# A vision tower's block on one core: gathers issued ahead of GpSimd's adds and powers, second norms' statistics ahead of the low parts, the biases' load in four parts

## The chip, the cores and the metric

One core of one Trainium2 chip runs the kernel as one launch. The metric is the device time of one execution in microseconds (us). The engines are TensorE (PE), VectorE (DVE), ScalarE (ACT), GpSimd (POOL) and SyncE (SP), which only issues transfers here. Times with a decimal such as 541.53 are moments, in us from the start of the profiled span.

## The reference

```python
h = L0_tok_ref(x, ...)                       # 8 x 256 x 512, a state space model's kernel
h = concat([cls_tok, h], axis=1)             # 8 batches of 257 rows of 512
h = h + attention(layernorm(h), ...)         # 16 heads of 32
h = h + ffn(layernorm(h), ...)

def ffn(x, router_w, router_b, expert_w, expert_b, out_w, out_b):
    probs = softmax(x @ router_w + router_b)            # 8 experts
    top, idx = top_k(probs, 2); top = top / top.sum()
    expert_out = gelu(x @ expert_w[e] + expert_b[e])    # for every e, 512 x 512
    combined = sum over the two chosen experts of gate * expert_out
    return combined @ out_w + out_b
```

Only the two chosen experts of a row matter, so the kernel computes those alone.

## The kernel before

The kernel makes the tokens, runs attention for 8 batches one after another, and then the experts. Rows are kept as 17 token tiles of 128 rows: two halves for each of 8 batches, and one class tile whose first 8 rows are the class rows. Matrix products in float32 precision are made of three passes of TensorE: an operand is split into a high part (a rounded copy, made by ScalarE) and a low part (the operand less its high part, made by VectorE); `ew_hi` and `ew_lo` are those of the experts' matrices, `xnT_hi` and `xnT_lo` those of a turned (transposed) tile.

**Slot tiles.** Each row appears twice, once for each of its experts, in a list sorted by expert and padded to 40 tiles of 128 slots. The kernel doesn't wait for the last two batches: the first 16 slot tiles (`FULL`) hold only rows of the first six batches, whose routing is done within attention's last batch. Then for slot tile i: GpSimd gathers its rows from `xn_dram` (`gather(i)`, L917) into one of two buffers, TensorE turns them (`turn_xs(i)`, L2492), ScalarE makes the high part (`hi_xs`, L1335), the low part comes from VectorE (`lo_xs`, L1999) for tiles 0, 1 and from 8 on and from ScalarE (`lo_xs`, L1346, out of a difference that TensorE makes, `rest_of_xs`, L2247) for tiles 2 to 7, TensorE multiplies by the expert's matrix (`expert(i)`, L2313), ScalarE applies gelu (L1356) and issues the store. For tiles 0 to 11 TensorE adds the expert's bias by a matmul (L2790) of picked rows of `bias_rows`; later tiles get it from VectorE out of `eb`, a copy of all biases on all partitions (2 MB, loaded by SyncE, L676). `bias_rows` itself comes from a small load `bias_rows_raw` (L670), ScalarE's high part (L1367) and VectorE's low part (L2023), followed by the picks (L2025).

**The late token tiles.** Tiles of the last two batches and the class tile (numbers 12 to 16 in TensorE's order) are finished beside the first slot tiles: VectorE adds attention's output (`residual`, L1669; class rows L2030), makes the second norm's statistics (`stats_of`, `norm_sums`, L1672 to L1678; class tile L2048 to L2052), GpSimd takes the power -1/2 (`norm_pow`, L895; class tile L938) and adds the output bias into `h_ob` (`last_bias`, L891; class tile L940) for SyncE to store (`keep_h`, L639; class tile L683), and VectorE normalises in place (`normalise`, L1684; class tile L2060), which must come behind that add. SyncE stores the normalised tiles (`keep_xn`, L644; class tile L685). TensorE turns them (`turn_xn`) behind expert tile 3, ScalarE copies them (`keep_xnT`, L1175), and routing of the rest follows from there, spread over slot tiles 4 to 14 by tile number. The low parts of experts 1 to 7 (`lo_expert`, L1995) are made by VectorE in between: expert 1's behind the statistics of batch 6, expert 2's behind the class tile's, expert 3's behind the normalising of batch 7, experts 4 to 7 at the end.

**What sets the order.** Every engine runs its own program in the order written, and semaphores are the only links. The lists that matter here:

- TensorE: turn 0, turn 1, expert 0, turn 2, expert 1, turn 3, expert 2, turn 4, expert 3, turns of late tiles 12 to 16, turn 5, expert 4, logits of the late tiles, turn 6, expert 5 and so on. In the middle of expert i (for i up to 6) comes `rest_of_xs(i + 1)`, which waits for ScalarE's high part of tile i + 1.
- GpSimd before: add for batch 6 (two), gathers 0 and 1, power of batch 6, gathers 2 and 3, adds for batch 7 (two), power of batch 7, class power, class add, two fills, gathers 4 to 39. A gather i waits until tile i - 2 is turned.
- ScalarE: high parts of tiles 0 and 1, high part of the bias rows, high parts of experts 5 to 7, gelu of tile 0; then for each tile i: high part of i + 1, store of i - 1, low part of i + 1, gelu of i. Behind gelu 3 it copies late tiles 12 to 15, waits for the stores out of `h_ob`, the class tile's among them, and copies tile 16, whose place overlaps `h_ob`; only then comes the high part of tile 5.

```python
                if i == 3:
                    for n in range(EARLY_TILES, NT - 1):
                        keep_xnT(n)
                    act.wait_ge(st_h[0], 16 * (NB + 2))
                    act.wait_ge(st_h[1], 16 * (NB + 1))
                    keep_xnT(NT - 1)
```

- SyncE: matrix of expert 7, `h_ob` of batch 7 (two stores), the biases `eb`, normalised tiles of batches 6 and 7 (four stores), class tile's `h_ob`, class tile's normalised rows. All of these use one queue.

Of the kernel before, what the change touches and what calls it, by code (L numbers as in the profile page):

```python
# [8 lines left out]
ALU = mybir.AluOpType  # L9
# [3 lines left out]
P = 128  # L13
BANK = 512
EPS = 1e-5
# [6 lines left out]
def vit_tower_kernel(nc, x, cls_tok, log_dt, B_ri, inv_A_real, A_imag, Wq, bq, Wk, bk, Wv, bv, Wo, bo,  # L22
# [69 lines left out]
    BIASES_BY_PE = 12  # L92
    DVE_KEPT = [sum(KEPT_BY_DVE[:n]) for n in range(NT + 1)]
# [15 lines left out]
    with ExitStack() as whole:  # L109
# [457 lines left out]
        def _(sp):  # L567
# [105 lines left out]
            for st in range(HALVES):  # L673
                keep_h(last, st)
            sp.wait_ge(s["dve_bias_rows"], 1)
            sp.dma_start(eb[:, :, :].rearrange("p e d -> p (e d)"),  # L676
                         expert_b.rearrange("e d -> (e d)").rearrange("(a n) -> a n", a=1).broadcast_to([P, NE * D])
                         ).then_inc(s["loaded_biases"], 16)
# [35 lines left out]
        def _(pool):  # L714
# [178 lines left out]
            def norm_pow(m):  # L893
                pool.wait_ge(s["dve_stats2"], 5 * m + 5)
                pool.tensor_tensor(rs2[:, 1, :], rs2[:, 0, :], mhalf[:, :], ALU.pow).then_inc(s["pool_rstd"], 1)  # L895
# [33 lines left out]
            for i in range(2):  # L929
                gather(i)  # L930
            norm_pow(last - 1)
            for i in range(2, 4):
                gather(i)
            for st in range(HALVES):
                last_bias(last, st)
            norm_pow(last)
            pool.wait_ge(s["dve_stats2"], 5 * NB + 3)
            pool.tensor_tensor(rsc[:, 1, :], rsc[:, 0, :], mhalf[:, :], ALU.pow).then_inc(s["pool_rstd"], 1)  # L938
            pool.wait_ge(st_h[0], 16 * (NB + 1))
            pool.tensor_tensor(h_ob[:, 0, :], tok[:, CLS, :], ob[:, :], ALU.add).then_inc(s["pool_out_bias"], 1)  # L940
            pool.wait_ge(s["pe_cls_projected"], 1)
# [3 lines left out]
            for i in range(4, FULL):  # L945
                gather(i)
# [19 lines left out]
        def _(act):  # L966
# [453 lines left out]
        def _(dve):  # L1420
# [250 lines left out]
            def residual_stats(m, st):  # L1671
                dve.bn_stats(st2[:, st, :], tok[:, st * NB + m, :]).then_inc(s["dve_stats2"], 1)  # L1672

            def norm_sums(m):
                for st in range(HALVES):
                    dve.bn_aggr(mv2[:, st, :], st2[:, st, :]).then_inc(s["dve_stats2"], 1)
                dve.wait_ge(s["dve_stats2"], 5 * m + 4)
                dve.tensor_scalar(rs2[:, 0, :], mv2[:, :, 1], EPS, None, ALU.add).then_inc(s["dve_stats2"], 1)  # L1678

            def normalise(m, st):  # L1680
# [1211 lines left out]
```

## Time and profile before

| | |
|---|---|
| median of 3 runs | 752.23 us (751.95 to 752.47) |
| profiled execution, as timed | 749.79 us |
| its span in the profile | 748.0 us |
| TensorE busy | 675.2 us, 90% of the span |
| VectorE busy | 526.9 us, 70% |
| ScalarE busy | 417.1 us, 56% |
| GpSimd busy | 158.0 us, 21% |
| granted TensorE clock, mean | 0.977 of full speed |

The profiled execution is one of its own, timed at 749.79 us, 2.44 less than the median of the runs; all moments in this document are within its span of 748.0 us. A row of a timeline gives the start, the duration (of all instructions merged in it, if it says x2 or more), the engine, the line, the operation, what it writes and reads, and in brackets how long the engine was idle before it and what ended that. L917 is line 917 of the kernel. Matmuls are pipelined, so the distance between two starts says more than a duration.

### The profile page before, as it was taken

To read this page: it belongs to the slowest core of one execution; us is meant where nothing else is said; L and a number is where in the kernel's file an instruction comes from. 1 tells how busy PE (TensorE), PEld (TensorE's weight loads), DVE (VectorE), ACT (ScalarE), POOL (GpSimd) and SP (SyncE) were. 2 spreads that over 40 slices of the span, in tenths; PEclk is the share of its full clock that TensorE was granted. 3 is DMA by queue.
4 is the path that set the end of the run, shared out by engine and by line. 5 is a ranking of instruction groups with operands and counts; after the bars stand their busy time and mean duration, and the time that the engine had idled before them with its cause. 6 is when DMAs were issued, how large, how long until landed. Compare 5 with 4: busy or idle time off the path is not lost.

```text
span 748.0 us, 16610 instructions
## 1 busy us (share of the span) xinstructions
PE 675.2 (90%) x5699; PEld 539.0 (72%) x5700; DVE 526.9 (70%) x1240; ACT 417.1 (56%) x1077; POOL 158.0 (21%) x310
## 2 busy tenths in 40 slices
PE   4788988879999999999999999796769989998998
PEld 3577877768777787877778787564557778886886
DVE  7999883657777787787878777867842744446775
ACT  5864644577767676676667667755433423334111
POOL 5200000110120201212111120111822232236660
PEclk9889999989999999999999999999889999999999
DMA  7501255300000010000001002426543356666895
GB/s 204 193 1 29 114 143 143 72 1 2 3 29 28 14 42 0 28 28 28 28 14 42 0 28 86 169 71 218 187 172 120 120 151 208 202 188 207 262 331 173
DMA packets 54684, 76.29 MB, mean 102 GB/s; under 512 B 24729, under 2 KB 27033, under 8 KB 54514
## 3 DMA queue, kind: packets, MB, share of 16 engines
q1 hardware_dynamic: 40978, 42.56, 17.8%
q0 software_dynamic: 5920, 19.40, 9.4%
q10 hardware_dynamic: 7744, 13.77, 5.0%
q8 instruction: 26, 0.43, 0.2%
q14 instruction: 16, 0.13, 0.1%
HBM read 45.55 MB, written 30.16 MB: 101 GB/s over the span
## 4 chain that ended last, share of the span: by engine, by line
PE 68%; DVE 16%; ACT 5%; issue 4%; DMA 3%; POOL 2%; ACTq 0%; DVEq 0%; POOLq 0%; SPq 0%
PE ps L2313 41%; PE ps L2419 8%; PE ps L2429 4%; PE ps L2412 4%; PE ps L2492 3%; DVE ring L1578 3%; DVE ring L1577 3%; ACT prb L1135 2%; PE ps L2260 1%; DMA rows_in<-xn_dram,token_of 1%; PE ps L2436 1%; PE ps L2291 1%; DVE prb L1657 1%; PE ps L2304 1%; PE ps L2379 1%
## 5 line engine op out<-in xcount | busy, mean ns | idle before, releaser
L1135 ACT ACTIVATE prb<-ps,negmax 128x257 f32<-128x257 f32 x256 | 117.7, 479 | 4.7 <-DVE negmax L1648 3.7
L1648 DVE TENSOR_REDUCE negmax<-ps 128x2 f32<-128x514 f32 x128 | 82.4, 685 | 13.5 <-PE ps L2412 13.5
L2419 PE MATMUL ps<-ident,prb 128*128 128x128 f32 x512 | 83.4, 286 | 9.4 <-DVE prb L1657 3.4
L2419 PEld LDWEIGHTS ps<-ident,prb 128*128 128x128 f32 x512 | 57.0, 143 | 33.9 <-issue 10.7
L1657 DVE TENSOR_SCALAR prb<-prb,rrec 128x258 f32<-128x258 f32 x256 | 73.5, 351 | 2.3
L2313 PE MATMUL ps<-ew_hi,xnT_hi 128*128 x160 | 68.5, 428 | 3.9 <-DVE xnT_lo L1999 3.4
L1356 ACT ACTIVATE rows_out<-ps 128x512 f32<-128x512 f32 x40 | 23.9, 598 | 79.0 <-DVE ps L2068 60.2
L2313 PE MATMUL ps<-ew_lo,xnT_hi 128*128 x160 | 64.7, 404 | 0.0
L2313 PE MATMUL ps<-ew_hi,xnT_lo 128*128 x160 | 64.3, 402 | 0.0
L917 POOL DMA_INDIRECT rows_in<-xn_dram,token_of x40 | 40.7, 1018 | 107.9 <-PE ps L2492 88.9
L1999 DVE TENSOR_TENSOR xnT_lo<-ps,xnT_hi 128x512 fp32r<-128x512 f32 x34 | 23.5, 690 | 55.9 <-ACT xnT_hi L1335 55.7
L1143 ACT ACTIVATE pts_far<-ps 128x512 f32<-128x512 f32 x64 | 38.6, 604 | 41.8 <-PE ps L2419 41.8
L2260 PE MATMUL ps<-ident,ring 128*128 128x128 f32 x384 | 49.3, 286 | 7.3 <-DVE ring L1578 7.2
L1135 ACT ACTIVATION_READ_ACCUMULATOR prb<-ps,negmax 128x1 f32 x256 | 53.9, 211 | 0.0
L2260 PEld LDWEIGHTS ps<-ident,ring 128*128 128x128 f32 x384 | 44.9, 148 | 11.5 <-DVE ring L1578 11.2
L2492 PE MATMUL ps<-ident,rows_in 128*128 128x128 f32 x228 | 35.5, 279 | 16.5 <-DMA rows_in<-xn_dram,token_of 13.4
L1654 DVE RECIPROCAL rrec<-rowsum 128x4 f32<-128x4 f32 x64 | 11.4, 178 | 52.8 <-ACT prb L1135 52.5
L2492 PEld LDWEIGHTS ps<-ident,rows_in 128*128 128x128 f32 x228 | 27.4, 142 | 25.7 <-DMA rows_in<-xn_dram,token_of 13.6
L848 POOL TENSOR_TENSOR pcls<-prb,ones 128x12 f32<-128x12 f32 x40 | 8.4, 209 | 149.4 <-DVE prb L1657 149.4
L2313 PEld LDWEIGHTS ps<-ew_hi,xnT_hi 128*128 128x128 f32 x160 | 31.5, 197 | 10.8 <-issue 5.1
L2313 PE MATMUL ps<-xT_hi,wqT_hi 128*128 128x258 f32 x128 | 38.7, 303 | 0.0
L959 POOL DMA_INDIRECT y_rows<-y_slots,slot_of x34 | 34.8, 1024 | 17.7 <-DVE rows_in L2209 10.5
(480 smaller groups left out, 1812.3 us busy)
## 6 DMA issues: line engine op xcount, KB each, us to landing
y_slots<-rows_out ACTq DMA_DIRECT2D x40, 256.0 KB, 3.4
ew<-in_L_ffn_expert_w_dram SPq DMA_DIRECT2D x8, 1024.0 KB, 5.5
h_dram<-h_ob SPq DMA_DIRECT2D x17, 256.0 KB, 2.0
xn_dram<-tok SPq DMA_DIRECT2D x17, 256.0 KB, 2.2
h_late<-h_dram SPq DMA_DIRECT2D x12, 256.0 KB, 4.5
out_dram<-h_late SPq DMA_DIRECT2D x11, 256.0 KB
y_slots<-u_sb SPq DMA_DIRECT2D x9, 256.0 KB, 5.7
tok_dram<-so SPq DMA_DIRECT2D x4, 512.0 KB, 3.2
```

The source lines that it names most:

```text
L917: pool.indirect_dma_start(out=rows_in[:, i % 2, :], out_offset=None, in_=xn_dram[0:rows, :], in_offset=bass.IndirectOffsetOnAxis(ap=token_ ...
L959: pool.indirect_dma_start(out=y_rows[:, t % Y_RING, k, :], out_offset=None, in_=y_slots, in_offset=bass.IndirectOffsetOnAxis(ap=slot_of[:, ...
L1135: e = act.activation(prb[:, u % 2, j, 0:KEYS], ps[:, j, 0:KEYS], ACT.Exp, bias=negmax[:, u % 2, j:j + 1], accum_out=rowsum[:, u % 2, j:j + 1])
L1143: act.activation(pts(slot, 2)[:, :, :, st * P:(st + 1) * P], ps[:, 4, :].rearrange("p (h t s) -> p h t s", h=2, t=HALVES), ACT.Copy).then_ ...
L1648: dve.tensor_reduce(negmax[:, u % 2, 2 * b:2 * b + 2], ps[:, 2 * b:2 * b + 2, 0:KEYS], AX_X, ALU.max, negate=True).then_inc(s["dve_max"], 1)
L1657: e = dve.tensor_scalar(prb[:, u % 2, j, :], prb[:, u % 2, j, :], rrec[:, u % 2, j:j + 1], None, ALU.mult)
L2260: mm = pe.matmul(ps[:, n % 4, q * P:(q + 1) * P], part(q), ident[:, :], is_transpose=True, start=(k == 0 and q == 0), stop=(k == len(parts ...
L2313: mm = pe.matmul(out_ap, a, b, start=start and i == 0, stop=stop and i == 2, skip_group_check=skip)
L2412: mm = pe.matmul(ps[:, j, 0:KPAD], a[rows, ci, st * P:(st + 1) * P], b[rows, ci, :], start=(a is q_hi and b is k_hi), stop=(b is k_lo))
L2419: mm = pe.transpose(ps[:, 4, (2 * j + tt) * P:(2 * j + tt + 1) * P], prb[:, u % 2, 2 * b + j, tt * P:(tt + 1) * P], ident[:, :])
L2429: mm = pe.matmul(ps[j * DH:(j + 1) * DH, bank, 0:KEYS], v_sb[:, tt, h * DH:(h + 1) * DH], pts(h)[:, 0, tt, 0:KEYS], start=(tt == 0), stop= ...
L2492: mm = pe.matmul(ps[:, bank, k * P:(k + 1) * P], src[:, k * P:(k + 1) * P], ident[:, :], is_transpose=True, start=(k == 0), stop=(k == KC ...
```

## The change

- GpSimd issues gathers 2 and 3 directly behind 0 and 1, then does batch 7's adds, then both batches' powers and the class power; gathers 4 and 5 follow ahead of the class add, 6 and 7 behind it, ahead of the two fills. The class add now waits for `dve_attn_done` itself.
- Batch 7's statistics get tiles of their own (`lnst`, `lnmv`, `lnr`), so that they needn't wait for batch 6's normalising.
- VectorE makes the low parts of tiles 0 and 1 (and adds the class rows) ahead of the biases' low part and the picks; then the statistics of batch 6, of batch 7 and of the class tile; then the low parts of experts 1 to 7; then it normalises batch 6, batch 7 and the class tile.
- ScalarE makes the high part of the bias rows ahead of tiles 0 and 1.
- SyncE loads `eb` in four parts of two experts each; part n (from 0) waits until n + 3 slot tiles are turned.

```diff
+    BIASES_AT_ONCE = 2
...
             sp.wait_ge(s["dve_bias_rows"], 1)
-            sp.dma_start(eb[:, :, :].rearrange("p e d -> p (e d)"),
-                         expert_b.rearrange("e d -> (e d)").rearrange("(a n) -> a n", a=1).broadcast_to([P, NE * D])
-                         ).then_inc(s["loaded_biases"], 16)
+            for e in range(0, NE, BIASES_AT_ONCE):
+                sp.wait_ge(s["pe_slot_turned"], 3 + e // BIASES_AT_ONCE)
+                some = expert_b[e:e + BIASES_AT_ONCE, :].rearrange("e d -> (e d)").rearrange("(a n) -> a n", a=1)
+                sp.dma_start(eb[:, e:e + BIASES_AT_ONCE, :].rearrange("p e d -> p (e d)"),
+                             some.broadcast_to([P, BIASES_AT_ONCE * D])).then_inc(s["loaded_biases"], 16)
...
             pool.wait_ge(s["dve_token_of"], 1)
-            for i in range(2):
-                gather(i)
-            norm_pow(last - 1)
-            for i in range(2, 4):
+            for i in range(4):
                 gather(i)
             for st in range(HALVES):
                 last_bias(last, st)
-            norm_pow(last)
+            norm_pow(last - 1)
+            norm_pow(last, lnr)
             pool.wait_ge(s["dve_stats2"], 5 * NB + 3)
             pool.tensor_tensor(rsc[:, 1, :], rsc[:, 0, :], mhalf[:, :], ALU.pow).then_inc(s["pool_rstd"], 1)
+            gather(4)
+            gather(5)
             pool.wait_ge(st_h[0], 16 * (NB + 1))
+            pool.wait_ge(s["dve_attn_done"], 1)
             pool.tensor_tensor(h_ob[:, 0, :], tok[:, CLS, :], ob[:, :], ALU.add).then_inc(s["pool_out_bias"], 1)
+            gather(6)
+            gather(7)
             pool.wait_ge(s["pe_cls_projected"], 1)
...
-            for i in range(4, FULL):
+            for i in range(8, FULL):
                 gather(i)
...
+            act.wait_ge(s["loaded_biases"], 16 * 2 * DH // NE)
+            act.activation(bias_rows[0:2 * DH, :], bias_rows_raw[0:2 * DH, :], ACT.Copy).then_inc(s["act_w_high"], 1)
             act.wait_ge(s["dve_expert_of"], 1)
             hi_xs(0, 0, True)
             hi_xs(1, 1, True)
-            act.wait_ge(s["loaded_biases"], 16 * 2 * DH // NE)
-            act.activation(bias_rows[0:2 * DH, :], bias_rows_raw[0:2 * DH, :], ACT.Copy).then_inc(s["act_w_high"], 1)
...
             for st in range(HALVES):
                 residual(last, st, 2 + st)
+            lo_xs(0, 0)
+            dve.wait_ge(s["loaded_cls"], 16)
+            dve.wait_ge(s["pe_cls_projected"], 1)
+            dve.tensor_tensor(tok[0:NB, CLS, :], ps[0:NB, 6, :], tok[0:NB, CLS, :], ALU.add).then_inc(s["dve_attn_done"], 1)
+            lo_xs(1, 1)
             dve.wait_ge(s["act_w_high"], KC * KC + 1)
...
-            lo_xs(0, 0)
-            dve.wait_ge(s["loaded_cls"], 16)
-            dve.wait_ge(s["pe_cls_projected"], 1)
-            dve.tensor_tensor(tok[0:NB, CLS, :], ps[0:NB, 6, :], tok[0:NB, CLS, :], ALU.add).then_inc(s["dve_attn_done"], 1)
-            lo_xs(1, 1)
...
-            stats_of(last - 1)
-            norm_sums(last - 1)
-            lo_expert(1)
-            for st in range(HALVES):
-                normalise(last - 1, st)
-            stats_of(last)
-            dve.wait_ge(s["dve_xn"], 2 * last)
-            norm_sums(last)
+            stats_of(last - 1, own_sums)
+            dve.wait_ge(s["dve_stats2"], 5 * last)
+            stats_of(last, last_sums)
+            dve.wait_ge(s["dve_stats2"], 5 * NB)
             dve.wait_ge(s["dve_attn_done"], 1)
             dve.bn_stats(stc[:, :], tok[:, CLS, :]).then_inc(s["dve_stats2"], 1)
...
-            lo_expert(2)
+            for e in range(1, NE):
+                lo_expert(e)
             for st in range(HALVES):
-                normalise(last, st)
-            lo_expert(3)
+                normalise(last - 1, st, own_sums)
+            for st in range(HALVES):
+                normalise(last, st, last_sums)
             dve.wait_ge(s["pool_rstd"], NB + 1)
             dve.wait_ge(s["pool_out_bias"], NT)
             dve.tensor_scalar(tok[:, CLS, :], tok[:, CLS, :], mvc[:, 0:1], rsc[:, 1, 0:1], ALU.subtract, ALU.mult
                               ).then_inc(s["dve_xn"], 1)
-            for e in range(4, NE):
-                lo_expert(e)
...
-            dve.wait_ge(s["loaded_biases"], 16 * 2 * DH // NE + 16)
+            dve.wait_ge(s["loaded_biases"], 16 * 2 * DH // NE + 16 * NE // BIASES_AT_ONCE)
```

## Rows read from the trace of the kernel before

**Rows 1.** The page: its first line, and one line of the transfers issued.

```profile
span 748.0 us, 16610 instructions
...
h_dram<-h_ob SPq DMA_DIRECT2D x17, 256.0 KB, 2.0
```

**Rows 2.** The chain that ended last, 510 to 565 us: start, us, what.

```profile
525.90 2.70 POOL rs L895
...
534.73 2.66 POOL rsc L938
537.39 3.72 POOL h_ob L940
...
541.53 6.20 DMA rows_in<-xn_dram,token_of
```

**Rows 3.** Timeline of TensorE.

```profile
523.19 0.79 PE L2313 MATMUL ps<-ew_hi,xnT_hi 128*128 x1 [2.96 <-DVE xnT_lo L1999]
...
547.77 1.12 PE L2492 MATMUL ps<-ident,rows_in 128*128 128x128 f32 x4 [5.44 <-DMA rows_in<-xn_dram,token_of]
...
554.49 1.10 PE L2492 MATMUL ps<-ident,tok 128*128 128x128 f32 x8
...
557.80 0.60 PE L2492 MATMUL ps<-ident,rows_in 128*128 128x128 f32 x4
...
561.53 0.49 PE L2790 MATMUL ps<-bias_rows,picks 64*128 64x512 f32 x1
```

**Rows 4.** Timeline of VectorE.

```profile
521.41 0.68 DVE L2023 TENSOR_TENSOR bias_rows<-bias_rows_raw,bias_rows 32x512 fp32r<-32x512 f32 x1 [4.71 <-ACT bias_rows L1367]
...
529.62 1.28 DVE L1672 BATCH_NORM_STATS2 st<-tok 128x6 f32<-128x512 f32 x2
...
531.21 2.42 DVE L1678 TENSOR_SCALAR rs<-mv 128x2 f32<-128x2 f32 x1
...
534.55 2.29 DVE L1995 TENSOR_TENSOR ew_lo<-ew,ew_hi 128x2048 fp32r<-128x2048 f32 x1
536.75 1.00 DVE L1684 TENSOR_SCALAR tok<-tok,mv,rs 128x512 f32<-128x512 f32 x2
537.66 2.29 DVE L1995 TENSOR_TENSOR ew_lo<-ew,ew_hi 128x2048 fp32r<-128x2048 f32 x1
...
541.67 8.89 DVE L1995 TENSOR_TENSOR ew_lo<-ew,ew_hi 128x2048 fp32r<-128x2048 f32 x4
```

**Rows 5.** Timeline of ScalarE.

```profile
520.27 0.60 ACT L1335 ACTIVATE xnT_hi<-ps 128x512 fp32r<-128x512 f32 x1 [0.77 <-PE ps L2492]
...
521.28 5.50 ACT L1248 ACTIVATE ew_hi<-ew 128x2048 fp32r<-128x2048 f32 x3
526.80 1.28 ACT L1356 ACT_TABLE_LOAD   x1
...
558.08 0.60 ACT L1175 ACTIVATE xnT_cls<-ps 128x512 f32<-128x512 f32 x1 [0.40 <-PE ps L2492]
```

**Rows 6.** Timeline of GpSimd.

```profile
530.12 0.95 POOL L917 DMA_INDIRECT rows_in<-xn_dram,token_of  x1 [0.30 <-issue]
531.10 2.50 POOL L891 TENSOR_TENSOR h_ob<-tok,ob 128x512 f32<-128x512 f32 x2
...
537.35 3.75 POOL L940 TENSOR_TENSOR h_ob<-tok,ob 128x512 f32<-128x512 f32 x1
...
542.96 1.83 POOL L917 DMA_INDIRECT rows_in<-xn_dram,token_of  x1 [0.30 <-issue]
```

**Rows 7.** Stretches: length, then each engine's busy time, granted clock, DMA share, GB/s.

```profile
512.00:514.00 2.00, 0.84 (x25) 0.77 (x26) 1.90 (x11) 1.22 (x1) 0.00 (x0) 1.00 1.04 395
...
548.00:550.00 2.00, 2.00 (x7) 1.54 (x7) 2.00 (x2) 0.60 (x1) 0.84 (x1) 0.50 0.15 58
```

**Rows 8.** Timeline of SyncE's queue.

```profile
534.00 0.45 SPq L676 DMA_DIRECT2D eb<-in_L_ffn_expert_b_dram  x1
```

**Rows 9.** Line 683, the class tile's store of h, issued at 541.13: time to landing.

```profile
DMA to landing us min/median/max: 6.5/6.5/6.5
```

More of the change, by code:

```diff
@@ L891, in add_bias, with norm_pow @@
                 pool.tensor_tensor(h_ob[:, st, :], tok[:, st * NB + m, :], ob[:, :], ALU.add).then_inc(s["pool_out_bias"], 1)
-            def norm_pow(m):
+            def norm_pow(m, sums=rs2):
                 pool.wait_ge(s["dve_stats2"], 5 * m + 5)
-                pool.tensor_tensor(rs2[:, 1, :], rs2[:, 0, :], mhalf[:, :], ALU.pow).then_inc(s["pool_rstd"], 1)
+                pool.tensor_tensor(sums[:, 1, :], sums[:, 0, :], mhalf[:, :], ALU.pow).then_inc(s["pool_rstd"], 1)
             body(0, True)
@@ L1669, in residual, with residual_stats, norm_sums, normalise @@
                 dve.tensor_tensor(t, ps[:, bank, :], t, ALU.add).then_inc(s["dve_residual"], 1)
-            def residual_stats(m, st):
-                dve.bn_stats(st2[:, st, :], tok[:, st * NB + m, :]).then_inc(s["dve_stats2"], 1)
-            def norm_sums(m):
+            own_sums, last_sums = (st2, mv2, rs2), (lnst, lnmv, lnr)
+            def residual_stats(m, st, sums=own_sums):
+                dve.bn_stats(sums[0][:, st, :], tok[:, st * NB + m, :]).then_inc(s["dve_stats2"], 1)
+            def norm_sums(m, sums=own_sums):
                 for st in range(HALVES):
-                    dve.bn_aggr(mv2[:, st, :], st2[:, st, :]).then_inc(s["dve_stats2"], 1)
+                    dve.bn_aggr(sums[1][:, st, :], sums[0][:, st, :]).then_inc(s["dve_stats2"], 1)
                 dve.wait_ge(s["dve_stats2"], 5 * m + 4)
-                dve.tensor_scalar(rs2[:, 0, :], mv2[:, :, 1], EPS, None, ALU.add).then_inc(s["dve_stats2"], 1)
-            def normalise(m, st):
+                dve.tensor_scalar(sums[2][:, 0, :], sums[1][:, :, 1], EPS, None, ALU.add).then_inc(s["dve_stats2"], 1)
+            def normalise(m, st, sums=own_sums):
                 dve.wait_ge(s["pool_out_bias"], 2 * m + st + 1)
@@ L1683, in normalise @@
                 t = tok[:, st * NB + m, :]
-                dve.tensor_scalar(t, t, mv2[:, st, 0:1], rs2[:, 1, st:st + 1], ALU.subtract, ALU.mult
+                dve.tensor_scalar(t, t, sums[1][:, st, 0:1], sums[2][:, 1, st:st + 1], ALU.subtract, ALU.mult
                                   ).then_inc(s["dve_xn"], 1)
@@ L2026, in _, with stats_of @@
                               ALU.is_equal).then_inc(s["dve_bias_rows"], 1)
-            lo_xs(0, 0)
-            dve.wait_ge(s["loaded_cls"], 16)
-            dve.wait_ge(s["pe_cls_projected"], 1)
-            dve.tensor_tensor(tok[0:NB, CLS, :], ps[0:NB, 6, :], tok[0:NB, CLS, :], ALU.add).then_inc(s["dve_attn_done"], 1)
-            lo_xs(1, 1)
-            def stats_of(m):
+            def stats_of(m, sums):
                 for st in range(HALVES):
                     dve.wait_ge(s["dve_residual"], HALVES * m + 1 + st)
-                    residual_stats(m, st)
+                    residual_stats(m, st, sums)
                 dve.wait_ge(s["dve_stats2"], 5 * m + 2)
-            stats_of(last - 1)
-            norm_sums(last - 1)
-            lo_expert(1)
-            for st in range(HALVES):
-                normalise(last - 1, st)
-            stats_of(last)
-            dve.wait_ge(s["dve_xn"], 2 * last)
-            norm_sums(last)
+                norm_sums(m, sums)
+            stats_of(last - 1, own_sums)
+            dve.wait_ge(s["dve_stats2"], 5 * last)
+            stats_of(last, last_sums)
+            dve.wait_ge(s["dve_stats2"], 5 * NB)
             dve.wait_ge(s["dve_attn_done"], 1)
```

## The prediction

> **What bounds the kernel now.** I read the chain of waits first, then each engine's timeline in the stretch where attention ends and the expert tiles begin, then the transfers. The profiled execution spans 748.0 us [rows 1]. From 563 us on, the chain is TensorE with pauses that hang on tile numbers; what is decided before that point shifts the end by itself. Up to 563 the chain isn't TensorE: it goes through GpSimd, whose power waits for VectorE's statistics and runs 2.70 us, whose class power runs 2.66 and whose class add runs 3.72, and then through gather 4, which takes 6.20 from its issue at 541.53 to TensorE's turn [rows 2]. TensorE stands idle for 5.44 in front of that turn, at 547.77. Tile 0 also starts late, at 523.19 after 2.96 of idleness, for want of its low part [rows 3]; VectorE makes that only after the biases' low part of 521.41, for which it had waited 4.71 [rows 4].
>
> I use one mark: the end of expert tile 4. Its bias matmul starts at 561.53 and the next work comes 0.42 later: **561.95** [rows 3]. The gain at the mark is the gain at the end.
>
> **Part 1, gathers first.** Gather 2 needs only that tile 0 is turned, and was held by the power until 528.6 [rows 2]. Now gathers 2 and 3 go at about 519.0 and 520.5 (tile 1 was turned by 520.2, since ScalarE copied it at 520.27 [rows 5]) and land before TensorE asks. Each costs GpSimd 0.95. Their price is that the last two adds, 2.50 together [rows 6], now sit at 521.5 to 524.0.
>
> **Part 2, the biases' copy ahead of the tiles' high parts on ScalarE, the tiles' low parts ahead of the biases' on VectorE.** The bias rows' small loads stood behind two matrices that still ran at 395 GB/s between 512 and 514 [rows 7]; I count them as there by 516, so the copy (0.6) fits in before tile 0 is turned at 518.8. Were they 2 us later, tile 0's high part would slip by up to 0.6, which the slack below swallows. Tile 0 then starts near 520.4, 2.8 earlier. Tile 1's second half needs tile 2's high part, and ScalarE comes to that only after three matrices (5.50, from 520.8), a table load (1.28) [rows 5] and one copy: 528.7. So tile 1 ends near 531 and tile 2 near 534.6. Tile 3 needs gather 4, which now stands behind the class power: about 537. It ends near 541.2, against 554.49 before [rows 3]: 13 us won so far. It doesn't last.
>
> **Part 3, statistics first, then all seven low parts, then the normalising.** TensorE's next work behind tile 3 is to turn the five late token tiles, which must be normalised; VectorE now does that after the low parts of experts 1 to 7. VectorE is ready for the biases' low part at 521.5, the very moment at which GpSimd's adds start. What a meeting costs: a 128x2 operation issued at 531.21 took 2.42, until GpSimd's two adds of 531.10 were over [rows 4, 6]. I take the like of it: free at 524.0. Then the biases' low part and the picks, 0.8; two rounds of statistics at 1.7 (a pair of 1.28 and what follows, 529.62 to 531.21 and a last step); the class tile, 0.9 (533.63 to 534.55) [rows 4]. The low parts begin at **529.1**; without a meeting, at 526.7. Four low parts took 8.89 and one takes 2.29, so one follows another after 2.20 [rows 4]; seven take 15.5: **544.6**. The first normalised tile is 0.5 later (two take 1.00) [rows 4], 545.1. Five turns and that of slot tile 5 took from 554.49 to 558.40, 3.9. TensorE comes out of 4 us of idleness; behind such a pause one turn took 1.12 instead of 0.60 [rows 3] and the granted clock was 0.50, 1.2 GHz, in the stretch from 548 to 550 [rows 7]. I add 1.0 in all (bounds 0 and 2): tile 5 is turned at **550.0**.
>
> **Part 4, the biases' load in four parts.** The 2 MB load was issued at 534.00 [rows 8] and slowed everything behind it: the class tile's store of h took 6.5 [rows 9] where such a store takes 2.0 [rows 1]. The parts now wait for turned slot tiles 2 to 5, and SyncE's order is otherwise kept: part four, four normalised tiles, the class tile's h, its normalised rows. So **those five stores wait, with part four, for tile 5's turn at 550.0**. ScalarE waits for the class store of h before it copies the fifth late tile (the copy's place overlaps h_ob), and in its program the high part of slot tile 5 comes after that copy; TensorE needs that high part in the middle of expert tile 4. Before, this wait cost nothing: the store had landed at 547.6 (541.13 + 6.5) and the copy of 558.08 waited for its turn alone [rows 5, 9]. Now, from 550.0: 0.52 + 4 x 0.26 + 0.26 MB and gather 7's 0.26 are 2.1 MB, at 395 GB/s [rows 7] 5.3 us, and 1.7 for issue and start (a lone store of 0.26 MB lands in 2.0 [rows 1], 0.65 of it at that rate). That is 7.0: **557.0**. Bounds 5.0 (the rate alone) and 8.5. Two copies of 0.6 [rows 5]: 558.3. The rest of tile 4 takes 2.1 at the full clock (half of the 4.15 from 557.80 to the mark) and 3.4 at the low one (a turn and tile 3 took 6.7 behind a pause, 547.77 to 554.49, so 2.6 more, half of it here) [rows 3]; I take 2.8: **561.1**.
>
> **The sum.** 529.1 + 15.5 + 5.4 + 7.0 + 1.3 + 2.8 = 561.1 against 561.95: 0.85 off. The profiled execution took 749.79 as timed; the median of the runs is 752.23, 2.4 more, and I subtract from the median: **751.4**. The early gain is nearly all given back.
>
> **Bounds of the sum.** Low: no meeting (2.4), transfers in 5.0 (2.0), full clock (0.7 and 1.0): 745.3. High: the class add gets in between two low parts and holds VectorE for 1.25 (half of 2.50 [rows 6]), the class power for 0.6 (it ended at 537.39, behind a low part that ended at 536.84 [rows 2, 4]), transfers 8.5, low clock 0.6 more: 755.3.
>
> **A rule of the skill against the trace.** Two rows show who waits at the port that VectorE and GpSimd share. The class add of 537.35 took 3.75, until 1.15 behind the end of a low part that started after it, at 537.66: it was passed over. Gather 5, issued at 542.96 during a low part, ended at 544.79, 0.9 behind the start of the next one at 543.87 (541.67 + 2.20) [rows 4, 6]: it got in. The Trainium skill, SBUF — State Buffer, "Who interferes with whom", says that a VectorE instruction with two SBUF inputs and a GpSimd one that reads SBUF exclude each other and that whoever issues first gets the ports, and it infers that a tensor_tensor doesn't hold up a gather's descriptors. By it a waiting power is let in at the next boundary, the third rival below has no chance, and the time is 751.4. The trace agrees on the exclusion, not on the order; and for the gather it shows 1.83 instead of 0.95 where the page infers no wait.
>
> **Rivals.**
> 1. *SyncE's order doesn't reach TensorE.* If the class store landed in time, tile 4 would run from 550.0 and end near 554: 8 gained, **744.2**. For it: the wait never showed before. Against it: the order of the queue and of ScalarE's program. Chance 0.10.
> 2. *The same chain, but short:* GpSimd's adds miss VectorE (526.7) and the transfers take 6: **748.0**. For it: the two starts at 521.5 are within 0.1 of each other. Chance 0.17.
> 3. *The class power starves behind seven low parts, and gather 4 with it.* The power is issued just as the first low part begins, as at 534.73, where it took 2.66 [rows 2]. There it got in behind one low part; the add of 537.35 was passed over at its first boundary. Held until VectorE rests at 546.5: power 547.2, gather 4 issued by 548.4 and landed at 551.0, tile 3 until 555.2, turns 559.1, transfers 566.1, mark 570.2: 8.2 lost, **760.4**. TensorE wants gather 4 by 540.9 (4.2 ahead of 545.1), so this decides from a power that ends later than 537, behind the third low part. Chance 0.10. The milder case (the class add and a power let in between low parts, a slow queue: **755**) has 0.10 more.
> 4. *The change doesn't do what it says:* the stalls trade places exactly, within 1 us of **752.2**. Chance 0.08.
>
> **How the numbers follow.** A measurement of this kernel can tell about 0.2%, 1.5 us, from no change. My case has 0.45; its own range is 748.8 to 753.8, with 0.16 faster, 0.24 within, 0.05 slower. Rivals 1 and 2 add 0.27 to faster, rival 3 and its milder case 0.20 to slower, rival 4 0.08 to the same. Together: faster 0.43, same 0.32, slower 0.25. The range leaves out rival 1 and the starved case (0.20) and ends at the bounds, 745.3 and, rounded up, 756.
>
> **What would show it.** Right: gather 2 near 519 and no wait of 5 us for a gather at tile 3; VectorE with seven low parts in a row from 527 to 529; TensorE idle for about 4 us ahead of the late tiles' turns and again for 4 to 6 in the middle of expert tile 4, released by ScalarE's high part, which sits behind the copy that waits for the class store; SyncE's part four right behind tile 5's turn near 550. Wrong: no pause inside tile 4 (rival 1), a bias low part of 0.68 at 521.5 (rival 2), a class power of more than 8 us (rival 3). A mark under 555 or over 566 would mean that I follow the wrong chain.

## The result and the profile after

The median of 6 runs is **755.8 us** (754.46 to 757.23) against 752.09 for the kernel before in the same session (751.15 to 752.62, 6 runs): ratio **1.005, interval 1.0037 to 1.0063**. The change made the kernel 3.7 us slower; the forecast was 751.4 and somewhat faster. The profiled execution took 757.23, with a span of 755.5.

How TensorE waited tells the story in two answers. The list of TensorE's waits, before (514 to 562 us) and after (517 to 568); columns: who waited, for what, us in total, times, longest:

```profile
PE ps L2492 <- DMA rows_in<-xn_dram,token_of: 11.6, 4, 5.4
PE ps L2313 <- DVE xnT_lo L1999: 3.0, 1, 3.0
```

```profile
PE ps L2252 <- ACT xnT_hi L1341: 8.7, 2, 7.8
PE ps L2497 <- DVE tok L1692: 3.5, 1, 3.5
PE ps L2497 <- DMA rows_in<-xn_dram,token_of: 2.8, 2, 2.1
PE ps L2795 <- DVE picks L2038: 1.1, 1, 1.1
```

The waits for gathers fell from 11.6 to 2.8 and the one for a low part from 3.0 to 0.5. In their place stand 3.5 for the normalised tiles and 8.7 for a high part, 7.8 of it in one piece. The lines shown add up to 14.6 before and 16.1 after.

The chain that ended last, after:

```profile
524.71 2.98 DVE bias_rows L2036
...
534.68 7.88 DVE ew_lo L2003 x4
542.56 2.02 issue
544.58 4.48 DVE ew_lo L2003 x2
549.06 0.47 DVE tok L1692
...
551.07 3.57 PE ps L2497 x16
554.66 0.33 SPq L680
...
557.06 5.60 DMA h_dram<-h_ob
...
563.18 0.60 ACT xnT_hi L1341
```

GpSimd, which carried the chain before [rows 2], is gone from it; the 2.02 called issue at 542.56 lie within a low part that began at 541.28 and that GpSimd's class add had held up. The chain runs over VectorE's low parts, the late turns, SyncE's part four (554.66), the class tile's store and ScalarE's high part: the forecast's path, in the forecast's order. TensorE's timeline shows the moments on it:

```profile
523.85 0.49 PE L2318 MATMUL ps<-ew_hi,xnT_hi 128*128 x1 [0.53 <-DVE xnT_lo L2007]
...
540.26 0.85 PE L2497 MATMUL ps<-ident,rows_in 128*128 128x128 f32 x4 [2.14 <-DMA rows_in<-xn_dram,token_of]
...
549.66 1.07 PE L2497 MATMUL ps<-ident,tok 128*128 128x128 f32 x8 [3.47 <-DVE tok L1692]
...
553.82 0.81 PE L2497 MATMUL ps<-ident,rows_in 128*128 128x128 f32 x4
...
563.82 0.80 PE L2252 MATMUL ps<-xnT_hi,nident 128*128 128x512 f32 x1 [7.80 <-ACT xnT_hi L1341]
...
567.11 0.79 PE L2795 MATMUL ps<-bias_rows,picks 64*128 64x512 f32 x1
```

These answer to [rows 3]. Tile 3's turn, 547.77 before, is at 540.26, and the late turns, 554.49 before, at 549.66. Then, in the middle of tile 4, TensorE stands idle for 7.80. The mark (end of tile 4) is at 567.83. VectorE, ScalarE, GpSimd and SyncE [rows 4, 5, 6, 8, 9], one timeline each, then the landing of the class store (line 686):

```profile
524.71 2.98 DVE L2036 TENSOR_TENSOR bias_rows<-bias_rows_raw,bias_rows 32x512 fp32r<-32x512 f32 x1
...
532.48 16.58 DVE L2003 TENSOR_TENSOR ew_lo<-ew,ew_hi 128x2048 fp32r<-128x2048 f32 x7
```

```profile
562.68 0.60 ACT L1181 ACTIVATE xnT_cls<-ps 128x512 f32<-128x512 f32 x1 [9.04 <-DMA h_dram<-h_ob]
```

```profile
524.56 2.57 POOL L894 TENSOR_TENSOR h_ob<-tok,ob 128x512 f32<-128x512 f32 x2
...
532.64 2.66 POOL L939 TENSOR_TENSOR rsc<-rsc,mhalf 128x2 f32<-128x2 f32 x1 [0.45 <-DVE rsc L2057]
535.48 2.38 POOL L920 DMA_INDIRECT rows_in<-xn_dram,token_of  x1 [0.17 <-issue]
538.16 1.82 POOL L920 DMA_INDIRECT rows_in<-xn_dram,token_of  x1 [0.30 <-issue]
540.01 2.49 POOL L944 TENSOR_TENSOR h_ob<-tok,ob 128x512 f32<-128x512 f32 x1
542.65 2.83 POOL L920 DMA_INDIRECT rows_in<-xn_dram,token_of  x1 [0.15 <-issue]
```

```profile
529.16 25.83 SPq L680 DMA_DIRECT2D eb<-in_L_ffn_expert_b_dram  x4
555.03 1.99 SPq L645 DMA_DIRECT2D xn_dram<-tok  x4
557.06 0.43 SPq L686 DMA_DIRECT2D h_dram<-h_ob  x1
```

```profile
DMA to landing us min/median/max: 5.6/5.6/5.6
```

SyncE's fourth part ends its issue at 554.99, behind tile 5's turn; the class store waits its turn behind it and four stores of normalised tiles, and lands at 562.66. ScalarE's copy of the fifth late tile has waited 9.04 for that and starts at 562.68. The high part of tile 5, which TensorE wants, is next in ScalarE's program.

Stretches of after: length, busy time of TensorE, its weight loads, VectorE, ScalarE and GpSimd, granted clock, DMA share, GB/s.

```profile
551.00:553.00 2.00, 1.93 (x9) 1.66 (x10) 0.34 (x1) 1.01 (x2) 0.00 (x0) 0.50 0.00 0
...
555.00:557.00 2.00, 1.02 (x5) 0.50 (x3) 0.00 (x0) 0.00 (x0) 1.15 (x3) 1.00 0.67 152
...
559.00:561.00 2.00, 0.00 (x0) 0.00 (x0) 0.00 (x0) 0.00 (x0) 0.00 (x0) 1.00 1.03 398
561.00:563.00 2.00, 0.00 (x0) 0.00 (x0) 0.00 (x0) 0.32 (x1) 0.00 (x0) 0.52 0.80 307
...
565.00:567.00 2.00, 2.00 (x6) 1.17 (x4) 0.00 (x0) 0.25 (x1) 0.00 (x0) 0.50 0.04 8
...
612.00:614.00 2.00, 2.00 (x6) 1.55 (x6) 0.69 (x1) 0.24 (x1) 0.82 (x1) 0.57 0.59 172
```

The DMA engines are full only from 557 on. TensorE comes out of the pause with the granted clock at 0.50, which is 1.2 GHz, and the rest of tile 4 takes 4.0 (563.82 to 567.83). The last line is a later place where that clock shows.

**Where the time went.** The profiled executions differ by 7.5 us, more than the medians. I split each span at the start of gather 0 and at the mark:

| | ahead of gather 0 | gather 0 to mark (stage) | mark to end (tail) | span |
|---|---|---|---|---|
| before | 514.47 | 47.48 | 186.05 | 748.0 |
| after | 517.51 | 50.32 | 187.67 | 755.5 |
| before, second profile (e8) | 514.75 | 47.49 | 185.96 | 748.2 |
| after, second profile (e11) | 515.35 | 50.30 | 187.65 | 753.3 |

The stage and the tail repeat within 0.1. What lies ahead of gather 0 does not (512.6 to 517.6 over all thirteen profiles), and the change edits no instruction there; I take it for scatter (the section on e8 and e11 says how far that is shown). So the change costs **2.8 in the stage and 1.6 in the tail**. That is 4.4 to 4.5 in two profiles of each kernel, against 3.7 by the medians.

The 1.6 of the tail have one place. The distance from the turn of tile 16, which stands behind the wait for its gather (1.8 us in both kernels), to the next turn is 3.72 before (605.00 to 608.72) and 5.31 after (610.95 to 616.26). In after the granted clock fell to 0.57 there, as the last line above shows. TensorE's timelines, before and after:

```profile
605.00 0.66 PE L2492 MATMUL ps<-ident,rows_in 128*128 128x128 f32 x4 [1.75 <-DMA rows_in<-xn_dram,token_of]
```

```profile
610.95 0.66 PE L2497 MATMUL ps<-ident,rows_in 128*128 128x128 f32 x4 [1.80 <-DMA rows_in<-xn_dram,token_of]
```

### The profile page after: what moved, and what is told of

The parts are those of the page before. It is cut to its first block, busy times and chain, and to the rows that moved or that the text cites. A ratio compares the mean times of both kernels' runs of the same rounds, so it can differ in the third digit from the quotient of the medians.

```text
span 755.5 us, 16616 instructions
## 1 busy us (share of the span) xinstructions
PE 679.7 (90%) x5699; PEld 540.7 (72%) x5700; DVE 528.0 (70%) x1240; ACT 417.5 (55%) x1077; POOL 157.6 (21%) x310
## 4 chain that ended last, share of the span: by engine, by line
PE 68%; DVE 18%; ACT 5%; issue 4%; DMA 3%; POOL 1%; ACTq 0%; SPq 0%; DVEq 0%; POOLq 0%
PE ps L2318 41%; PE ps L2424 8%; PE ps L2434 4%; PE ps L2417 4%; PE ps L2497 4%; DVE ring L1583 3%; DVE ring L1584 3%; ACT prb L1141 2%; DVE ew_lo L2003 2%; PE ps L2441 1%; PE ps L2265 1%; PE ps L2296 1%; DVE prb L1663 1%; PE ps L2309 1%; PE ps L2384 1%
## 5 line engine op out<-in xcount | busy, mean ns | idle before, releaser
L920 POOL DMA_INDIRECT rows_in<-xn_dram,token_of x40 | 42.5, 1063 | 118.8 <-PE ps L2497 100.2
L2265 PE MATMUL ps<-ident,ring 128*128 128x128 f32 x384 | 47.7, 280 | 6.7 <-DVE ring L1584 6.7
L2265 PEld LDWEIGHTS ps<-ident,ring 128*128 128x128 f32 x384 | 43.0, 143 | 11.0 <-DVE ring L1584 10.7
L2497 PEld LDWEIGHTS ps<-ident,rows_in 128*128 128x128 f32 x228 | 27.5, 142 | 16.5 <-DMA rows_in<-xn_dram,token_of 5.6
L2318 PE MATMUL ps<-xT_hi,wkT_hi 128*128 128x258 f32 x128 | 39.0, 305 | 0.0
```

The costliest lines, as they stand in the source:

```text
L920: pool.indirect_dma_start(out=rows_in[:, i % 2, :], out_offset=None, in_=xn_dram[0:rows, :], in_offset=bass.IndirectOffsetOnAxis(ap=token_ ...
L2265: mm = pe.matmul(ps[:, n % 4, q * P:(q + 1) * P], part(q), ident[:, :], is_transpose=True, start=(k == 0 and q == 0), stop=(k == len(parts ...
L2318: mm = pe.matmul(out_ap, a, b, start=start and i == 0, stop=stop and i == 2, skip_group_check=skip)
L2497: mm = pe.matmul(ps[:, bank, k * P:(k + 1) * P], src[:, k * P:(k + 1) * P], ident[:, :], is_transpose=True, start=(k == 0), stop=(k == KC ...
```

## The experiments

Each ran beside the kernel before on the same chip; stage, tail and tile 16 are read from one profiled execution of each, the medians from 4 to 10 runs. The edits are against the kernel after unless it says "before". Nothing is left out of the computation in any. Medians and ratios (with interval) are against the kernel before of the same session, whose medians were 751.88 (e1 to e4), 751.77 (e5 to e8) and 751.47 (e9 to e11). The last column is the distance at tile 16.

| kernel | median | ratio | stage | tail | tile 16 |
|---|---|---|---|---|---|
| before | 752.09 | 1 | 47.48 | 186.05 | 3.72 |
| after | 755.80 | 1.0050 | 50.32 | 187.67 | 5.31 |
| e1 before, load in four parts | 757.28 | 1.0079 (1.0051 to 1.0106) | 54.25 | 186.65 | 3.71 |
| e2 no waits for the parts | 744.42 | 0.9902 (0.9877 to 0.9928) | 41.02 | 187.23 | 5.03 |
| e3 parts last | 746.76 | 0.9930 (0.9911 to 0.9950) | 41.45 | 186.16 | 3.71 |
| e4 normalising first | 747.68 | 0.9949 (0.9927 to 0.9971) | 42.68 | 187.69 | 5.31 |
| e5 both of these | 738.78 | 0.9836 (0.9805 to 0.9867) | 33.98 | 186.17 | 3.72 |
| e6 before, GpSimd's order | 747.29 | 0.9947 (0.9928 to 0.9966) | 42.45 | 185.73 | 3.71 |
| e7 e5, adds behind the picks | **736.17** | 0.9803 (0.9781 to 0.9825) | 33.55 | 185.98 | 3.72 |
| e9 class store first | 751.56 | 1.0004 (0.9982 to 1.0026) | 46.47 | 187.48 | 5.25 |
| e10 waits one tile earlier | 745.75 | 0.9919 (0.9894 to 0.9943) | 40.41 | 187.83 | 5.25 |

The theory: two orders bind in a row, VectorE's (seven low parts ahead of the normalising) and SyncE's (stores behind part four, which waits for tile 5's turn). Rivals: the waits cost nothing and the low parts do it all; the size of the load does it, not its wait; or the pause inside tile 4 comes of something else on ScalarE.

### e1: the four-part load alone, on the kernel before

```diff
+    BIASES_AT_ONCE = 2
...
-            sp.dma_start(eb[:, :, :].rearrange("p e d -> p (e d)"),
...
+            for e in range(0, NE, BIASES_AT_ONCE):
+                sp.wait_ge(s["pe_slot_turned"], 3 + e // BIASES_AT_ONCE)
...
```

> The kernel before with the four-part load of the biases alone, waits and all. The queue theory (the class tile's store of h waits on SyncE behind part four, part four waits for tile 5's turn, and ScalarE's high part of tile 5 waits for that store): tile 5's turn stays at 558.4, the store lands about 8.0 later, then 1.2 for copies and about 4 for the rest of tile 4, mark near 571.5 against 561.95, less what a lighter queue gives gather 4 (up to 2.5): 7 to 10 us slower, 759 to 762, with a pause of 6 to 8 us inside expert tile 4. The VectorE theory (the loss is in the low parts ahead of the normalising): no loss from this part, 752 or a little less.

Slower by 5.4 us in the median, 2 to 5 us less than expected; the stage is 6.8 longer, just under the expected 7 to 10, and the pause inside tile 4 is 7.98, as expected. SyncE's and ScalarE's timelines:

```profile
559.64 0.43 SPq L686 DMA_DIRECT2D h_dram<-h_ob  x1
```

```profile
565.61 0.60 ACT L1178 ACTIVATE xnT_cls<-ps 128x512 f32<-128x512 f32 x1 [9.12 <-DMA h_dram<-h_ob]
```

The same pause stands in a kernel whose VectorE and GpSimd orders are untouched. The split also brings something: with no 2 MB in the way, gather 4 was on TensorE 3.5 after its issue (543.61 to 547.12) instead of 6.2 [rows 2].

### e2: the parts without their waits

```diff
-                sp.wait_ge(s["pe_slot_turned"], 3 + e // BIASES_AT_ONCE)
```

> The changed kernel with its four loads issued at once, without waiting for turned tiles. Queue theory: the class store goes out when the class add is done, ten us ahead of its use, the pause of 7.8 us inside expert tile 4 is gone and with it the low clock behind it: 8 to 10 us faster than the changed kernel, 746 to 748. VectorE theory: the wait of 3.5 us for the late tiles is what costs, and it stays: 754 to 756.

The pause inside tile 4 is gone and the stage is 9.3 shorter. So the pause comes with the wait, not with the size of the load. The wait of 4.69 for the normalised tiles stays, as the theory says. The median is 2 to 4 us below what was expected. One link of the expectation was wrong: the class store didn't go out when the class add was done (542.50), ten us ahead of its use, but behind the four stores of normalised tiles, which wait for VectorE:

```profile
551.37 0.56 SPq L685 DMA_DIRECT2D h_dram<-h_ob  x1
```

It landed 2.9 later, at 554.27, and ScalarE's copy started at 554.54. So with the seven low parts ahead of the normalising this store is almost late even without any wait on the load.

### e3: the parts kept, with their waits, behind the class tile's stores

```diff
-            for e in range(0, NE, BIASES_AT_ONCE):
...
             sp.dma_start(xn_dram[CLS * P:, :], ...
...
+            for e in range(0, NE, BIASES_AT_ONCE):
...
```

> The changed kernel with its four loads, waits kept, moved behind the class tile's normalised rows on SyncE. Queue theory: as the run without waits, 746 to 748; up to 1 us better than that one if 2 MB beside gathers 4 and 5 cost anything, since these lie ahead of a wait for VectorE anyway I expect no difference. VectorE theory: 754 to 756.

As expected: with waits and loads both there, only their place in SyncE's queue is different, and 8.9 us leave the stage. That tells the order of the queue from the wait as such. ScalarE still waits 0.48 for the class store, which is here issued at 551.26 behind the four stores.

### e4: the seven low parts behind the normalising, SyncE as in after

```diff
-            for e in range(1, NE):
-                lo_expert(e)
             for st in range(HALVES):
                 normalise(last - 1, st, own_sums)
...
+            for e in range(1, NE):
+                lo_expert(e)
```

> The changed kernel with VectorE's low parts of experts 1 to 7 behind the normalising of the late tiles, SyncE as changed. Queue theory: the pause inside tile 4 stays at 6 to 8 us, but its start moves forward with tile 5's turn, by the 3.5 us that TensorE waited for VectorE and what gather 4 gains: 750 to 752. VectorE theory: all of the loss and more comes back, 744 to 747, and no pause inside tile 4 is left.

Better than expected by 2 to 4 us. TensorE's timeline:

```profile
544.34 0.60 PE L2497 MATMUL ps<-ident,rows_in 128*128 128x128 f32 x4
...
554.35 0.79 PE L2252 MATMUL ps<-xnT_hi,nident 128*128 128x512 f32 x1 [7.86 <-ACT xnT_hi L1341]
```

Tile 5's turn moves from 36.3 to 28.7 behind the start of gather 0 (553.82 less 517.51; 544.34 less 515.63), and the pause, 7.86, stays whole. Its length doesn't hang on VectorE; when it starts does.

### e5: e3 and e4 together

> The changed kernel with both: the low parts of experts 1 to 7 behind the normalising, and the four-part load behind the class tile's normalised rows on SyncE. Queue theory: tile 5's turn ends 29.3 us behind the start of gather 0, as with the normalising first alone, and tile 4 runs right behind it in about 4: mark 33 us behind gather 0's start where the kernel before has 47.5. 12 to 14 us faster than before, 738 to 740. If something next in line (low parts of VectorE for tile 8, the routing of the rest) takes over: 742 to 745.

The stage is 16.34 shorter than after's; e3 and e4 alone took 8.87 and 7.64, which is 16.5. **The two stalls are in series and add.** 738.78 is as expected. With both orders mended, what is left of the change, read off the medians, is worth 13 us against the kernel before.

### e6: GpSimd's order alone, on the kernel before (gathers 4 to 7 around the class add as in after)

```diff
-            for i in range(2):
-                gather(i)
-            norm_pow(last - 1)
-            for i in range(2, 4):
+            for i in range(4):
                 gather(i)
             for st in range(HALVES):
                 last_bias(last, st)
+            norm_pow(last - 1)
             norm_pow(last)
...
+            gather(4)
+            gather(5)
...
+            gather(6)
+            gather(7)
...
```

> The kernel before with GpSimd's new order alone: gathers 0 to 3 ahead of adds and powers, 4 and 5 ahead of the class add. Queue theory: with the biases in one load and without waits the class store goes out when the class add is done, so the gain of the gathers comes through: gather 4 lands near 539 instead of 547.8, tile 3 ends near 543 and the mark near 551 to 553: 8 to 11 us faster, 741 to 744, more than the changed kernel with its waits taken out, since VectorE's old order normalises the late tiles by 541. The rival (the gathers bring little without the new order of VectorE): 748 to 752.

747.29: the direction is as expected, the size 3 to 6 us short. GpSimd's and TensorE's timelines show why:

```profile
538.46 3.29 POOL L917 DMA_INDIRECT rows_in<-xn_dram,token_of  x1 [0.17 <-issue]
```

```profile
526.35 0.79 PE L2316 MATMUL ps<-ew_hi,xnT_hi 128*128 x1 [5.39 <-DVE xnT_lo L2002]
...
544.18 0.66 PE L2495 MATMUL ps<-ident,rows_in 128*128 128x128 f32 x4 [4.17 <-DMA rows_in<-xn_dram,token_of]
```

The adds, now early, met the biases' low part, which took 3.12 instead of 0.68 ahead of tile 0's low part. And gather 4, behind the class power, was issued only at 538.46, where I had it landing near 539, and then took 3.29 beside VectorE's low part (538.57 to 540.86). I had priced neither. The 2 MB load is not what held it: it was issued at 525.27, and the DMA engines moved 66 GB/s from 531 to 533 and 49 from 541 to 543.

### e7: e5, and the last adds held until the biases' low part and the picks are done

```diff
             for i in range(4):
                 gather(i)
+            pool.wait_ge(s["dve_bias_rows"], 2)
             for st in range(HALVES):
```

> As the kernel with the normalising first and the load last, but GpSimd's two adds of batch 7 wait for the biases' low part and the picks. The port theory (the two adds shut VectorE out, 2.95 us for a low part that takes 0.68 alone): the biases' low part takes 0.68, TensorE's wait of 1.1 in front of tile 0's bias goes, and the adds meet a 128x2 operation of the statistics instead; mark 0 to 1.1 us earlier, time the same within 1 us. If the 2.95 has another cause than the adds: it stays.

VectorE's timeline, e5 and then e7:

```profile
523.72 2.96 DVE L2036 TENSOR_TENSOR bias_rows<-bias_rows_raw,bias_rows 32x512 fp32r<-32x512 f32 x1
```

```profile
519.77 0.68 DVE L2037 TENSOR_TENSOR bias_rows<-bias_rows_raw,bias_rows 32x512 fp32r<-32x512 f32 x1
```

The meeting is gone: 0.68 instead of 2.96, and the adds meet a 128x2 operation of the statistics, which takes 1.14. Of the 2.3 us the stage keeps only 0.43, since TensorE then waits 2.54 for a high part from ScalarE where it waited 0.94 in e5. 736.17 is the best median of all, 2.0% below the kernel before; that it beats e5 by 2.6 I can't say from these runs, as the intervals overlap and most of the difference in the profiles lies ahead of gather 0.

### e8, e11: before and after once more

> The kernel before once more, for a second trace of it. The trace of before started gather 0 at 514.5, the changed kernels at 515.6 to 517.6, though nothing ahead of that point was changed. If that is scatter between executions, this one lies anywhere from 514 to 518; if the changed program is slower ahead of that point, it is 514.5 again.

> The changed kernel once more, for a second trace. In the stretch from gather 0 to the end of expert tile 4 it should repeat the first trace within 1 us (50.4). The start of gather 0, 517.5 in the first, should lie anywhere from 514 to 518 if the part ahead of the change scatters between executions.

Each is one profiled execution. Stage and tail repeat, as the first section shows; the pause inside tile 4 was 7.96 in e11. The start of gather 0 repeats for the kernel before (514.47, 514.75), which I had named as the sign of a changed program that is slower ahead of that point; it doesn't for the changed one (517.51, 515.35), and e7, changed as well, has 512.57. Against a slower program speak that and the medians: their 3.7 leaves nothing for a loss ahead of a stage and a tail that cost 4.4. Two profiles of each don't settle it.

### e9: the class store ahead of the four stores of normalised tiles

```diff
             for e in range(0, NE, BIASES_AT_ONCE):
...
+            sp.wait_ge(s["pool_out_bias"], NT)
+            sp.dma_start(h_dram[CLS], h_ob[:, 0, :]).then_inc(st_h[0], 16)
             for m in (last - 1, last):
...
-            sp.wait_ge(s["pool_out_bias"], NT)
-            sp.dma_start(h_dram[CLS], h_ob[:, 0, :]).then_inc(st_h[0], 16)
```

> The changed kernel with the class tile's store of h directly behind part four on SyncE, ahead of the four normalised tiles; the wait of part four for tile 5's turn is kept. If the pause inside expert tile 4 is made of the wait and of what the store queues behind: the four tiles of 0.26 MB (four issues of 0.5 and up to 2.6 of transfer) drop out, the store lands 3.5 to 4.5 earlier, the pause falls from 7.8 to 3.5 or 4 and the low clock behind it may go too: 3.5 to 5 us faster than the changed kernel, 750.5 to 752.5. If the contents don't matter and only the turn does: 755 to 756.

The store is issued 2.06 earlier behind part four (552.85; in e11, on the same chip, 554.91 behind a part four issued at the same 552.5), and lands in 4.3. The pause falls from 7.96 to 4.31 and the stage by 3.8. 751.56 is inside what was expected. So the queue's order and what shares the DMA engines with the store make about half of the pause. The low clock did not go: the granted clock was 0.57 from 558 to 562, and the rest of tile 4 took 3.7 (558.31 to 562.02) behind a pause of only 4.31.

### e10: one constant

```diff
-                sp.wait_ge(s["pe_slot_turned"], 3 + e // BIASES_AT_ONCE)
+                sp.wait_ge(s["pe_slot_turned"], 2 + e // BIASES_AT_ONCE)
```

> The changed kernel with one constant changed: the parts wait for turned tiles 1 to 4 instead of 2 to 5, so part four goes out at tile 4's turn, ahead of the late tiles. Queue theory: as with the parts last or without waits, no pause inside tile 4, 744 to 747. If any four-part load with waits costs something on the queue: 750 or more.

```profile
552.21 0.60 ACT L1181 ACTIVATE xnT_cls<-ps 128x512 f32<-128x512 f32 x1 [0.72 <-DMA h_dram<-h_ob]
```

With part four behind the turn of tile 4 instead of tile 5, the late tiles' stores no longer queue behind it: ScalarE's wait is 0.72 instead of 9.04, the stage 9.9 shorter, the median 745.75, as expected. One digit turns the change from 3.7 us slower to 5.7 faster than the kernel before.

## Why the prediction was wrong

The chain was right link by link; the time came out on the other side because three terms of the sum were sized too small, and because the end doesn't simply follow the mark. In its terms, with after's moments (3.04 less in before's frame):

| term | forecast | measured | off |
|---|---|---|---|
| low parts begin, behind the start of gather 0 | 14.63 | 14.97 | +0.34 |
| **seven low parts** | 15.5 | 16.58 | **+1.08** |
| end of the low parts to tile 5 turned | 5.4 | 5.55 | +0.15 |
| **to the landing of the class store** | 7.0 | 8.05 | **+1.05** |
| two copies | 1.3 | 1.15 | -0.15 |
| **rest of tile 4** | 2.8 | 4.0 | **+1.2** |
| sum | 46.63 | 50.3 | +3.7 |

With the tail's 1.6 that is 5.3 more than forecast; the medians show 4.4 more (755.8 against 751.4).

**Part 1 (gathers first) was right.** Gathers 2 and 3 went at 522.29 and 523.59, in before's frame 519.3 and 520.6 (forecast 519.0 and 520.5), the adds at 521.5 to 524.1 (521.5 to 524.0). TensorE's wait for gather 4 fell to 2.14. e6 shows this part worth 5.0 in the stage by itself.

**Part 2 was right:** tile 0's expert matmuls begin at 523.85, 520.8 in before's frame (forecast near 520.4).

**Part 3, the meeting:** forecast and there. The forecast held the biases' low part up for 2.5; it took 2.98 where it takes 0.68 alone, so 2.3. e7 removed it (0.68).

**Part 3, seven low parts: the first step that failed.** The sum took the low parts at 2.20 each and left the class add's meeting to the bounds ("gets in between two low parts and holds VectorE for 1.25"). It did get in: issued at 540.01, it ended at 542.50, and one low part took 3.37 instead of 2.28. In e4, e5 and e7, where no add falls among them, seven take 15.50, the forecast's figure. GpSimd's program had the class add right where VectorE would be in its low parts, so the add belonged in the sum and not in a bound.

**Part 4, the transfers: the second.** The forecast put the whole 2.1 MB at the rate of 395 GB/s, with 1.7 for issue and start. The rate was right (398 between 559 and 561), the start wasn't: four stores took SyncE 1.99 to issue, and between 555 and 557 the engines moved only 152. The volume was short too: by the windows some 2.26 MB had moved when the store landed (an estimate: 2 us each at 152, 323 and 398 GB/s, 1.66 at 307), against the 2.1 counted. The class tile's normalised rows, issued at 557.54, share the engines and aren't in the sum. How much each of the two cost isn't separated. The class store was issued at 557.06, 2.1 behind part four, and took 5.6. e9 shows the same from the other side.

**Part 4, the rest of tile 4: the third, and beyond both its bounds** (2.1 and 3.4). The high one was worked from 547.77 to 554.49, where TensorE came back to the full clock on the way. Behind 7.8 us of idleness the granted clock stood at 0.50 for all of the rest, and TensorE's matmuls came 0.43 apart instead of 0.23. It is 4.0 in e1 and in e4 too, 3.8 in e11, and 3.7 in e9 behind a pause of 4.31: the length that the forecast itself expected was enough to leave its bounds.

**"What is decided before that point shifts the end by itself"** failed as well: the tail grew by 1.6 at tile 16. I named no mechanism for it ahead, and its cause is open. It isn't the pause as such: e1 has the pause and 3.71 there, e2 and e10 have none and 5.0 to 5.3.

**The rivals.** Rival 1, that SyncE's order doesn't reach TensorE, fell; its price was good, for e2, e3 and e10, where the pause inside tile 4 is gone, took 744.4, 746.8 and 745.8 (forecast for that case 744.2). Rival 2 needs the adds to miss VectorE; they met. Rival 3 needs a class power of over 8 us: it took 2.66 and was let in at the first boundary. Its milder case, 755, with "the class add and a power let in between low parts, a slow queue", came nearest, and I had given it 0.10; but the nearness is in part luck. The add and the queue are there (1.1 each), the power cost VectorE nothing that shows (the low parts around it started 2.20 apart), and the rest is the clock in tile 4 (1.2) and the tail (1.6), which that case doesn't name. The high bound of the range has a slip as well: the turns' own bound (2 where 1.0 was taken) isn't in its sum. It didn't matter, for that term was off by 0.15. Of the three failing terms the low parts were taken at their cheapest and the other two near the middle of their bounds; each was a wait or a clock whose conditions the forecast had itself put in place (an add among low parts, a queue of six issues, a pause of 4 to 6 us), so each should have been taken at its dear end: 1.25, 1.5 and 0.6 more, 3.35 of the 3.7.

**Who gets the port.** The forecast said that the trace agrees with the exclusion and not with the order, and the runs bear that out without giving an order of their own. Let in at the next start of a VectorE instruction: the class power of 532.64 (2.66) and the class add of 540.01 (2.49), issued 2.0 and 1.3 ahead of it during a low part, and a gather of e1 issued 0.10 ahead (1.01 from 548.05, low part at 548.15). First at the port with hardly any lead: batch 7's adds, 0.15 ahead of the biases' low part in after (524.56, 524.71) and by the profile 0.06 behind it in e6 (522.19, 522.13), which ran at their usual 2.5 while VectorE took 2.98 and 3.12. Passed over: the class add of the kernel before (3.75 from 537.35, low part at 537.66 [rows 4, 6]) and of e1 (3.74 from 539.44, low part at 539.75), and gather 4 of e6 (3.29 from 538.46, low part at 538.57), all three issued while VectorE was normalising. So the lead alone doesn't decide, and what does isn't shown. The Trainium skill, SBUF — State Buffer, "Who interferes with whom", has whoever issues first get the ports: the two of after and the gather of e1 agree with it, and so do the adds of after; the three passed over don't. The page infers that a tensor_tensor doesn't hold up a gather's descriptors; here the gathers that after issued during VectorE's two-input low parts took 1.82 to 2.83, each until 0.90 to 0.98 behind the start of the next low part, against 0.94 to 0.96 for gathers 1 to 3 of after, which had no such low part beside them.

## What to carry to other kernels

When a load is given a wait so that it comes later, list everything behind it in the same queue and who waits for each: here a store that once had 10 us to spare became the last to land, and moving the load behind it, or its wait one tile earlier, was worth 9 to 10 us. Ask the same of the stores that stand there already: without the load's wait this one had 0.3 us to spare. When long operations of VectorE are put in a row, look at every GpSimd operation that falls among them. Each took longer itself here (the class power 2.66 against 0.93 in e5, gathers 1.82 to 2.83 against 0.95), and one of the five, the 128x512 add, held VectorE for 1.1; what is sure to meet belongs in the sum, not in the bounds. A forecast pause of TensorE also carries a price behind it: here 8 us of idleness made the next 2.1 us of work take 4.0, and 4.3 us of idleness made it take 3.7.

## What was not expected of the hardware

- **The granted clock at tile 16.** In after, e2, e4, e9, e10 and e11 it fell to 0.50 to 0.57 behind the wait for that tile's gather, 1.7 to 1.9 us in all thirteen profiles, and that tile took 5.0 to 5.3 instead of 3.7; in the other seven it stayed at 1.00. Within the two kernels profiled twice it repeats. What the six have in common that e3, e5, e6 and e7 lack isn't settled.
- **Scatter far ahead of the change.** Gather 0 started between 512.6 and 517.6 us, with no instruction edited ahead of it. The granted clock between 130 and 200 us differs too, from 0.90 to 0.98, but doesn't put the executions in order (0.92 where gather 0 started at 517.51, 0.90 where it did at 515.35), so the cause is open. The two profiles of after differ by 2.2 us in the span and by 0.02 in the stage: splitting the span near the first edited instruction is what made single profiles comparable.
- **The landing of one store of 256 KB** took 5.5 to 5.9 behind part four and four stores, 4.3 behind part four with the stores behind it, and 2.9 to 3.0 behind the four stores alone (e2, e3, e10), against 2.0 as the median over the program [rows 1].
